# Pacing the row gathers, inverting the routing permutation in bf16, and moving an activation table load in a mixture-of-experts layer

## The reference

```
x = layernorm(x + attention(x))                      # called x1 in the kernel
probs = softmax(x @ gate_w)                          # 1024 x 8
gate_score, gate_idx = top_k(probs, 2), scores divided by their sum
combine[t, e] = gate_score of expert e for token t, times alpha[e]
h = gelu(x @ fc1_w[e] + fc1_b[e])                    # 256 -> 256, per expert
y = h @ fc2_w[e] + fc2_b[e]
x = layernorm(x + sum over e of combine[t, e] * y)
```

## Time and profile before

| | us |
|---|---|
| runs, median of 3 (lowest to highest) | 154.54 (153.67 to 154.86) |
| the profiled execution, in all | 154.99 |
| its span, first to last instruction | 153.2 |
| busy in the span: TensorE products | 119.4 (78%) |
| busy: DVE | 69.8 (46%) |
| busy: ACT | 63.4 (41%) |
| busy: POOL | 50.9 (33%) |
| mean granted TensorE clock | 0.871 of full |

### The profile page before, as it was taken

The page is one execution under the profiler, slowest core; times in us unless marked ns, Lnnn a source line. Parts: engine busy times, 40 slices in busy tenths (PEclk is TensorE's granted clock), DMA queues, the critical chain, the costliest instruction groups (busy, mean ns, idle before and its releaser), DMA issues.

```text
span 153.2 us, 2179 instructions
## 1 busy us (share of the span) xinstructions
PE 119.4 (78%) x682; PEld 102.2 (67%) x682; DVE 69.8 (46%) x202; ACT 63.4 (41%) x156; POOL 50.9 (33%) x75
## 2 busy tenths in 40 slices
PE   7699997989789979993921999999999999910000
PEld 7488896868689979972720878888888888700000
DVE  0559785986817797182011333433322212210981
ACT  4346983454710000354003456656575453500271
POOL 2009993670000001787772000025254354340000
PEclk9999999999955696899598579999999999995555
DMA  4899999902320000233332000000211112117724
GB/s 124 194 369 409 381 348 348 295 15 81 121 76 0 0 0 0 75 103 103 103 103 68 0 0 4 0 34 34 73 36 68 68 39 71 68 68 258 290 101 173
DMA packets 10633, 18.00 MB, mean 118 GB/s; under 512 B 1205, under 2 KB 7550, under 8 KB 10366
## 3 DMA queue, kind: packets, MB, share of 16 engines
q1 hardware_dynamic: 9086, 13.67, 26.2%
q0 software_dynamic: 1536, 4.20, 8.5%
HBM read 13.67 MB, written 4.19 MB: 117 GB/s over the span
## 4 chain that ended last, share of the span: by engine, by line
PE 52%; DVE 11%; issue 10%; DMA 9%; POOL 8%; ACT 5%; SPq 3%; ACTq 0%; POOLq 0%; DVEq 0%
PE ps L1089 16%; PE ps L1077 15%; PE ps L1087 5%; DMA wq<-in_w_q_t 5%; PE ps L913 3%; PE ps L1041 3%; DMA gT_hi<-pair_rows 2%; PE ps L1060 2%; PE ps L981 2%; POOL x L358 2%; DVE acc L876 2%; DVE stats L881 2%; POOL x L357 2%; DMA pair_rows<-kv,scatter_i 2%; SPq L292 2%
## 5 line engine op out<-in xcount | busy, mean ns | idle before, releaser
L530 ACT ACTIVATE g<-ps,b_step 128x128 f32<-128x128 f32 x46 | 14.4, 364 | 36.2 <-PE ps L1077 23.5
L397 POOL DMA_INDIRECT pair_rows<-kv,scatter_i x16 | 15.6, 972 | 39.4 <-DVE kv L862 39.4
L1077 PEld LDWEIGHTS ps<-early,w_now 128*128 128x128 f32 x184 | 25.3, 201 | 4.3 <-issue 2.8
L1077 PE MATMUL ps<-early,w_now 128*128 (+1 forms) x184 | 25.9, 287 | 2.5 <-issue 2.4
L1089 PE MATMUL ps<-wres,g 128*128 x92 | 27.8, 428 | 0.0
L862 DVE SCALAR_TENSOR_TENSOR kv<-ps,w_step,kv 128x256 f32 x23 | 11.1, 483 | 34.0 <-PE ps L1089 33.2
L1089 PEld LDWEIGHTS ps<-wres,g 128*128 128x128 f32 x92 | 16.8, 203 | 4.7 <-issue 0.7
L913 PE MATMUL ps<-ones 128*128 128x128 f32 x102 | 18.2, 355 | 1.0 <-POOL ones L337 1.0
L546 ACT COPY w_now<-wres 128x512 f32 x23 | 14.0, 617 | 11.1 <-issue 11.1
L913 PEld LDWEIGHTS ps<-ones 128*128 128x128 f32 x102 | 17.3, 265 | 1.3 <-POOL ones L337 1.0
L390 POOL DMA_INDIRECT gT_hi<-x_rows,gather_i x8 | 8.5, 1063 | 28.2 <-DVE gather_i L816 26.1
(11 more groups left out here) (157 smaller groups left out, 194.7 us busy)
## 6 DMA issues: line engine op xcount, KB each, us to landing
wres<-in_expert_w SPq DMA_DIRECT2D x8, 512.0 KB, 9.6
early<-in_x_t SPq DMA_DIRECT2D x4, 256.0 KB, 6.0
acc<-in_x_tok SPq DMA_DIRECT2D x1, 1024.0 KB, 9.0
rT<-in_rope_t SPq DMA_DIRECT2D x1, 1024.0 KB, 10.3
x_rows<-x SPq DMA_DIRECT2D x4, 256.0 KB, 2.8
gT_hi<-pair_rows SPq DMA_DIRECT2D x2, 512.0 KB, 4.2
gT_lo<-pair_rows SPq DMA_DIRECT2D x2, 512.0 KB, 6.0
out<-z SPq DMA_DIRECT2D x4, 256.0 KB, 2.2
```

Source lines behind the costliest of these rows:

```text
L397: g_.indirect_dma_start(out=pair_rows[:, :], out_offset=bass.IndirectOffsetOnAxis(ap=scatter_i[:, i:i + 1], axis=0), in_=y_acc[:, i * D:(i ...
L530: a.activation(g[:, s % 2, m, :], two(H_BANK, s)[:, tile(m)], ACT.Gelu, bias=b1_step[:, s, m:m + 1]).then_inc(g_ok, 1)
L1077: last = nc.tensor.matmul(two(H_BANK, s)[:, tile(m)], w1_now[:, s % W1_SLOTS, k, tile(m)], x[:, tile(k)], start=k == 0, stop=k == KD - 1)
```

## The change

1. ACT: the dummy activation that loads the GELU table moves behind the copies of tiles 4 and 6.
2. `WARM_ROUTE` from (10, 12, 4, 14) to (7, 8, 8, 4).
3. The inversion goes in two parts, in bf16. `lane_hot` is bf16 now. First only numbers: lane, token tile and choice of each pair (`ids`, small integers that bf16 holds exactly), by one `tile_id` operation ahead of each `lane_hot`. `gather_i` = lane x 8 + tile, made right behind the product, ahead of the plan; `scatter_i` = 2 x gather_i + choice, later. The weights follow in a second set of 16 products, each float32 weight as a sum of three bf16 parts; these products stand on TensorE between x_across(1) and fc1(0), and DVE adds the three results.
4. The weights' operations (`wt`, `w_of`) move out of the chain ahead of the positions, behind the plan.
5. On DVE x_evict(0) comes ahead of the bias operations, x_evict(1) behind them, and x_evict(2) ahead of DVE's register loads. ACT loads 3 registers, copies three weights, then loads the other 20.
6. POOL: gather i from 4 on waits for xs_ok i - 2, the eviction of tile i - 3. The scatters wait for `scatter_ok`.

```diff
-WARM_ROUTE = (10, 12, 4, 14)
+GATHERED_FIRST = 4
+WARM_ROUTE = (7, 8, 8, 4)
...
-            g_.tensor_copy(values[:, :, 0], pair_id).then_inc(ids_ok, 1)
+            g_.tensor_copy(ids[:, :, 0], own_lane.to_broadcast([P, 2 * T])).then_inc(ids_ok, 1)
+            g_.tensor_copy(ids[:, :, 1], tile_no).then_inc(ids_ok, 1)
+            g_.tensor_copy(ids[:, :, 2], choice_no).then_inc(ids_ok, 1)
...
             for i in range(TS):
+                if i >= GATHERED_FIRST:
+                    pool.wait_ge(xs_ok, i - GATHERED_FIRST + 2)
                 gather(i)
+            pool.wait_ge(scatter_ok, 1)
             for i in range(TS):
                 scatter(i)
...
-            a.activation(table_unused[:, 0:1], eps[:], ACT.Gelu)
             x1_across(4)
             x1_across(6)
+            a.activation(table_unused[:, 0:1], eps[:], ACT.Gelu)
...
-            e_off = loaded(ACT_ENGINE, w_off, (E - 1) * D, "counts of E - 1 comparisons")
+            e_off = loaded(ACT_ENGINE, w_off, (E - 1) * D, "counts of E - 1 comparisons", 0, W1_SLOTS)
...
             for s in range(W1_SLOTS):
                 w1_copy(s)
+            e_off += loaded(ACT_ENGINE, w_off, (E - 1) * D, "counts of E - 1 comparisons", W1_SLOTS, STEPS)
...
-            dve.wait_ge(th_ok, 1)
-            v.tensor_scalar(wt[:, 0, :], th[:], 0.5, 0.5, ALU.mult, ALU.add)
-            step(v.tensor_scalar(wt[:, 1, :], th[:], -0.5, 0.5, ALU.mult, ALU.add))
-            dve.wait_ge(ids_ok, 1)
-            step(v.tensor_tensor(values[:, :, 1], wt[:].rearrange("p k t -> p (k t)"), alp_of[:], ALU.mult))
...
-            v.tensor_tensor(tile_val[:], tile_hot[:].unsqueeze(2).to_broadcast([P, 2 * T, 2, TS]),
-                            values[:].unsqueeze(3).to_broadcast([P, 2 * T, 2, TS]), ALU.mult).then_inc(tile_val_ok, 1)
+            dve.wait_ge(ids_ok, 3)
             for i in range(0, 2 * T, 4):
+                v.tensor_tensor(tile_id[:, i:i + 4, :, :], tile_hot[:, i:i + 4, :].unsqueeze(2).to_broadcast([P, 4, 3, TS]),
+                                ids[:, i:i + 4, :].unsqueeze(3).to_broadcast([P, 4, 3, TS]), ALU.mult).then_inc(tile_id_ok, 1)
                 v.tensor_tensor(lane_hot[:, i:i + 4, :], lane.unsqueeze(1).to_broadcast([P, 4, P]),
...
+            dve.wait_ge(th_ok, 1)
+            v.tensor_scalar(wt[:, 0, :], th[:], 0.5, 0.5, ALU.mult, ALU.add)
+            v.tensor_scalar(wt[:, 1, :], th[:], -0.5, 0.5, ALU.mult, ALU.add).then_inc(w_side, 1)
+
+            dve.wait_ge(inv_mm, 1)
+            lane_ps, tile_ps, choice_ps = (ps[:, INV_BANK, c * TS:(c + 1) * TS] for c in range(3))
+            v.tensor_scalar(slot_lane[:], lane_ps, float(T), None, ALU.mult).then_inc(route, 1)
+            steps[0] += 1
+            dve.wait_ge(route, steps[0])
+            v.tensor_tensor(gather_i[:], slot_lane[:], tile_ps, ALU.add).then_inc(idx_ok, 1)
...
-            dve.wait_ge(inv_mm, 1)
-            step(v.tensor_copy(scatter_i[:], ps[:, INV_BANK, 0:TS]))
-            v.tensor_scalar(gather_i[:], scatter_i[:], 1, None, ALU.logical_shift_right).then_inc(idx_ok, 1)
             v.tensor_scalar(y_off[:], tau_s[:], float(D), None, ALU.mult).then_inc(y_off_ok, 1)
-            step(v.tensor_scalar(odd_i[:], scatter_i[:], 1, None, ALU.bitwise_and))
-            v.tensor_scalar(first[:], odd_i[:], -1.0, 1.0, ALU.mult, ALU.add).then_inc(first_ok, 1)
+            v.tensor_scalar(first[:], choice_ps, -1.0, 1.0, ALU.mult, ALU.add).then_inc(first_ok, 1)
+            dve.wait_ge(idx_ok, 1)
+            v.scalar_tensor_tensor(out=scatter_i[:], in0=gather_i[:], scalar=2.0, in1=choice_ps,
+                                   op0=ALU.mult, op1=ALU.add).then_inc(scatter_ok, 1)
...
+            dve.wait_ge(w_side, 1)
+            w_step_of(v.tensor_tensor(w_of[:], wt[:].rearrange("p k t -> p (k t)"), alp_of[:], ALU.mult))
+            w_step_of(v.tensor_copy(w_parts[:, :, 0], w_of[:]))
+            w_step_of(v.tensor_tensor(w_rest[:, 0, :], w_of[:], w_parts[:, :, 0], ALU.subtract))
+            w_step_of(v.tensor_copy(w_parts[:, :, 1], w_rest[:, 0, :]))
+            w_step_of(v.tensor_tensor(w_rest[:, 1, :], w_rest[:, 0, :], w_parts[:, :, 1], ALU.subtract))
+            w_step_of(v.tensor_copy(w_parts[:, :, 2], w_rest[:, 1, :]))
+            v.tensor_tensor(tile_w[:], tile_hot[:].unsqueeze(2).to_broadcast([P, 2 * T, 3, TS]),
+                            w_parts[:].unsqueeze(3).to_broadcast([P, 2 * T, 3, TS]), ALU.mult).then_inc(tile_w_ok, 1)
+
             v.tensor_scalar(pick_b2[:], eps_s[0:BIAS_ROWS, :], row_e[0:BIAS_ROWS, :], None,
                             ALU.is_equal).then_inc(pick_ok, 1)
...
+            x_evict(0)
             plan_step(v.tensor_tensor(eps_hot[:], eps_s[:].unsqueeze(2).to_broadcast([P, STEPS, E]),
...
             v.reduce_sum(b1_step[:], b1_part[:], axis=AX_X).then_inc(b1_ok, 1)
-            v.tensor_copy(w_slot[:], ps[:, INV_BANK, TS:2 * TS])
...
-            x_evict(0)
             x_evict(1)
+            dve.wait_ge(w_mm, 1)
+            w_high, w_mid, w_low = (ps[:, W_BANK, c * TS:(c + 1) * TS] for c in range(3))
+            plan_step(v.tensor_copy(w_slot[:, 0, :], w_high))
+            plan_step(v.tensor_tensor(w_slot[:, 1, :], w_slot[:, 0, :], w_mid, ALU.add))
+            plan_step(v.tensor_tensor(w_slot[:, 0, :], w_slot[:, 1, :], w_low, ALU.add))
...
+            x_evict(2)
             dve.wait_ge(y_off_ok, 1)
             offs = loaded(DVE, y_off, (TS - 1) * D, "step less counts of experts begun, capped at the last tile")
...
             for s in range(STEPS + 1):
-                if 2 <= s + 2 < TS:
+                if 3 <= s + 2 < TS:
                     x_evict(s + 2)
...
-            pe.wait_ge(tile_val_ok, 1)
             for i in range(2 * T):
+                pe.wait_ge(tile_id_ok, i // 4 + 1)
                 pe.wait_ge(hot_ok, i // 4 + 1)
...
             x_across(0)
             x_across(1)
+            pe.wait_ge(tile_w_ok, 1)
+            for i in range(2 * T):
+                last = nc.tensor.matmul(ps[:, W_BANK, 0:3 * TS], lane_hot[:, i, :],
+                                        tile_w[:, i, :, :].rearrange("p a j -> p (a j)"),
+                                        start=i == 0, stop=i == 2 * T - 1)
+            last.then_inc(w_mm, 1)
```

More of the change, by code:

```diff
@@ L87, in table @@
             return tab[:, at[0] - n:at[0]]
-        before_me, lane, tile_start, pair_id = table(P), table(P), table(TS), table(2 * T)
+        before_me, lane, tile_start, tile_no, choice_no = table(P), table(P), table(TS), table(2 * T), table(2 * T)
         base_mask = table(E * E).rearrange("p (e f) -> p e f", e=E)
@@ L158, in layer_kernel @@
         tile_hot = sb("tile_hot", [P, 2 * T, TS])
-        values = sb("values", [P, 2 * T, 2])
-        tile_val = sb("tile_val", [P, 2 * T, 2, TS])
+        lane_hot = sb("lane_hot", [P, 2 * T, P], BF16)
+        ids = sb("ids", [P, 2 * T, 3], BF16)
+        w_of = sb("w_of", [P, 2 * T])
+        w_rest = sb("w_rest", [P, 2, 2 * T])
+        w_parts = sb("w_parts", [P, 2 * T, 3], BF16)
+        tile_id = sb("tile_id", [P, 2 * T, 3, TS], BF16)
+        tile_w = sb("tile_w", [P, 2 * T, 3, TS], BF16)
         scatter_i = sb("scatter_i", [P, TS], I32)
+        slot_lane = sb("slot_lane", [P, TS])
         gather_i = sb("gather_i", [P, TS], I32)
-        odd_i = sb("odd_i", [P, TS], I32)
         first = sb("first", [P, TS])
-        w_slot = sb("w_slot", [P, TS])
+        w_slot = sb("w_slot", [P, 2, TS])
         start_i = sb("start_i", [P, E], I32)
@@ L189, in layer_kernel @@
         xs = early
-        lane_hot = rT[:].rearrange("p a s -> p (a s)").rearrange("p (i c) -> p i c", i=2 * T)
         y_acc = kv[:].rearrange("p t d -> p (t d)")
@@ L225, in layer_kernel @@
             sem(n) for n in "ident0 ident_ok const_ok all_ones_ok earlier_ok ids_ok b2_hi_ok b2_ok".split())
-        lg_mm, route, gap_ok, th_ok, chosen_ok, pos_mm, tile_val_ok, hot_ok, inv_mm, idx_ok, first_ok, plan, w_off_ok, y_off_ok, pick_ok, b1_ok, w_step_ok = (
-            sem(n) for n in "lg_mm route gap_ok th_ok chosen_ok pos_mm tile_val_ok hot_ok inv_mm idx_ok first_ok plan w_off_ok y_off_ok pick_ok b1_ok w_step_ok".split())
+        lg_mm, route, gap_ok, th_ok, chosen_ok, pos_mm, tile_id_ok, hot_ok, inv_mm, idx_ok, scatter_ok, tile_w_ok, w_mm, first_ok, plan, w_off_ok, y_off_ok, w_side, pick_ok, b1_ok, w_step_ok = (
+            sem(n) for n in "lg_mm route gap_ok th_ok chosen_ok pos_mm tile_id_ok hot_ok inv_mm idx_ok scatter_ok tile_w_ok w_mm first_ok plan w_off_ok y_off_ok w_side pick_ok b1_ok w_step_ok".split())
         w1_now_ok, xs_mm, xs_ok, fc1_mm, g_ok, fc2_mm, acc0_ok, y_ok = (
@@ L267, in layer_kernel, with loaded @@
         X1T_BANK = (2, 3, 0, 2, 3, 0, 2, 3)
-        LG_BANK, POS_BANK, INV_BANK, WARM_BANK = 1, 4, 5, 6
+        LG_BANK, POS_BANK, INV_BANK, WARM_BANK, W_BANK = 1, 4, 5, 6, 4
         def x1T_before(t):
             return (t + 1) // 2, t // 2
-        def loaded(engine, row, most, reason):
```

(17 more changed lines are left out.)

13 lines of the change are left out of this document (9 added, 4 removed).

## The result

| | before | after |
|---|---|---|
| median of 4 runs each on one chip, us | 154.7 (153.67 to 155.13) | 140.67 (138.57 to 140.81) |
| ratio | | 0.9033, 95% interval 0.8896 to 0.9171 |
| profiled execution, us (span) | 154.99 (153.2) | 140.7 (138.8) |

The change is 9.7% faster, 14 us where 11 were forecast. Applied to the 154.54 of the prediction the ratio gives 139.6, just under its low end of 140. The ratio takes only the runs of each kernel that fell in its faster state (138.57 and 140.64 us of the four after); the medians alone would give 0.909 and 140.5.

What follows compares the result with a forecast made beforehand. TensorE work was 52% of the chain, with 10.7 us lost to apparently late semaphore increments. 2.3 us ahead of fc1(2) plus 9.0 behind it made 11.3 less than 154.99: 143.7, given as 143.5 (139.5 to 146; scored range 140 to 148.5).

Steps and rivals of the forecast that it cites:

- the half clock at the loop's start: TensorE, thin stretch from 56 on: slow end 62.6 taken for x_across(0), plus 1.2 us for one half-clock stretch before fc1(5).
- the weight products: Sixteen bf16 products between x_across(1) and fc1(0) on TensorE: cost 0.5 to 0.9 us; fc1(0) at 64.3, 1.7 earlier.
- fc1(2)'s distance: DVE around the first steps: fc1(2) keeps 6.3 us from the eviction of tile 0, so 70.0, 2.3 earlier.
- The stall: fc1(2) to fc1(5): back-to-back gathers make TensorE's semaphore increments late; pacing them saves 9.0 us behind fc1(2).
- Ahead of fc1(2): Routing, planning and first steps up to fc1(2): 2.3 us earlier in all.
- Table load: ACT's GELU table load moved behind the copy of tile 4: gates and logits 0.7 us earlier.
- Inversion: Routing inversion in bf16 on DVE and TensorE: net gain 1.5 us, so inv_mm 3.2 earlier, at 56.1.
- pick_ok and four warm rounds: TensorE ahead of x_across(0): pick_b2 ends 4.8 us from inv_mm, four rounds take 1.1 to 1.8; x_across(0) at 62.0 to 62.8.
- B: Rival, 7%: stall isn't the gathers' spacing, 152.5 us; elsewhere the machine condition with before at 145 to 147 us.
- A: Rival, 12%: pacing relieves only half the stall, 148.2 us; elsewhere the machine condition with before at 154 to 155 us.
- C: Rival, 4%, slower: late increments come with any gather in flight, and pacing stretches the flights; 160 us at 1.5 per gather.
- The rule on the SBUF port: DVE operations lock GpSimd out, so DMA descriptors come late: first gather could lose 2 to 3 us more, some 146 total.

Runs made afterwards that it cites:

- r_before: The kernel before, no edit, for its own trace in the condition where it takes 145 to 147 us: 146.11 us, ratio 1.0049.
- r_after2: The changed kernel, no edit, with more rounds, where the kernel before takes 145 to 147 us: 140.11 us, ratio to before 0.9614.
- r_after: The changed kernel, no edit, where the kernel before takes 145 to 147 us: 141.93 us, ratio to before 0.9828.
- e_table_back: The changed kernel with the dummy GELU activation ahead of ACT's copies of tiles 4 and 6 again: 141.81 us, ratio to before 0.9808.
- e_old_warm: The changed kernel with WARM_ROUTE back at (10, 12, 4, 14), where the kernel before takes 154 to 155 us: 145.09 us, ratio to before 0.9373.

## Why the prediction was right or wrong, point by point

**What put the number outside the range: the half clock at the loop's start.** fc1(5) was forecast at 79.1 and came at 75.75. Of these 3.35 us 1.6 lie behind fc1(2): I added 1.2 for a stretch at half clock and 0.5 for late gathers and evictions, and neither came. The other 1.8 are the balance of what lies ahead of fc1(2): 0.6 because pick_b2 ended earlier, 0.6 because the four warm-up rounds took 1.13 us where I took the slow end of 1.1 to 1.8, and 0.8 because the weight products ran under the eviction of tile 0, an overlap that I had put at nothing; less 0.2 in fc1(2)'s distance from fc1(0). "I take the slow end, 62.6, as TensorE has little to do from 56 on and its granted clock fell to half after other thin stretches" is the step that failed. The clock did stand at half, but from 55.5 to 59.0 us, ahead of the four rounds, and it was full from 59.0 through the whole start of the loop.

**The stall (the main term, 9.0 us).** For the two profiled executions the size holds: fc1(2) to fc1(5) shrank from 17.96 to 7.54 us, the remote waits beside the gathers are gone, and the gathers are released one by one. But I took a stall that needs the machine's condition for one of the kernel alone. The second step that failed is "My reading: back-to-back gathers cause the late increments", as a full cause. Back-to-back gathers aren't sufficient: r_before and three unpaced runs have them in B, and no stall. That in A they are what the increments are late for fits every trace taken there, down to the small delays beside the changed kernel's own short series; whether the pacing is the cure in A was never tested by itself. I call it argued, not shown. That the forecast came within 3 us of the result owes something to luck: the changed kernel was measured against runs in A, and in B the same change gains 2 to 4%. I saw nothing in the trace of one execution that told me; three runs within 1% of each other did not either, since they shared the condition.

I also read two standstills of TensorE as one stall. The first (69.84 to 72.26) is in r_before too, 2.29 us of waiting for the eviction of tile 2 behind DVE's register loads. Only the second, 6.1 us, and the 2.8 us of half clock behind it need A. The other 1.6 us of half clock, between the two, come in B as well.

**Ahead of fc1(2): 2.3 forecast, 4.05 measured.** The chain was right; sizes and one overlap were off.
- *Table load*, 0.7. The copy of tile 4 came 1.8 us earlier, and gate(4) ran at 41.52 still at full clock, 0.51 us instead of 1.02 at half. base_part came 2.9 earlier instead of 1.8. That this is the move's doing isn't shown: in B the gates end at different times from trace to trace (the first DVE operation on the logits at 42.93 in r_after2, 44.76 in r_before, 45.41 in r_after), with the clock, and e_table_back shows no difference.
- *Inversion*, 1.5. From base_part to gather_i before 8.17 us, after 7.11, so 1.1. The tile_id operations cost what I had (0.27 from start to start, forecast 0.25), and lane_hot in bf16 is not faster, as assumed (0.60 from start to start). The missing 0.4 lie behind them: the last four products ended 0.7 us behind the last lane_hot, where I had 0.3.
- *pick_ok and four warm rounds*, then the weight products. The chain was right: pick_b2 ended 4.9 us behind the inversion's product (4.8 forecast), and the rounds ran behind it. The sixteen products took 0.56 us, under the eviction of tile 0 (61.84 to 62.26). fc1(0) started 0.06 us behind that eviction, where I had added 0.5 to 0.9 for them. So fc1(0) came 3.7 us earlier and not 1.7.
- *fc1(2)'s distance* from the eviction of tile 0: 5.95 us instead of 6.33 (forecast 6.3). It waited 1.16 us for the eviction of tile 2, as described.

**The rivals.** B said that then only the gain ahead of fc1(2) remains. In condition B that is nearly what happens: 5.9 us, 4.2 ahead of fc1(2). Its cause as I gave it, that each gather costs as before, isn't it. The Trainium skill, "Runtime: NRT & Kernel Launch", section "Instruction fetch mechanics", was the rule behind it: r_before executes the same instructions without the stall, so fetching alone doesn't make it. A fetch even falls in that stretch in r_before (queue, packets, MB and share, from 66 to 84 us), where the trace before has none:

```profile
q8 instruction: 1, 0.02, 0.4%
```

A foresaw late increments where gathers and scatters are mixed. They are there in A, by 1.5 us beside the first scatters, but only around step 13 and at no cost; the 4.5 us of A are refuted. C, that any gather in flight makes increments late, is refuted: paced ones don't in A, and pacing costs nothing in B.

**The rule on the SBUF port** (the Trainium skill, "SBUF — State Buffer", section "SBUF: two separate sides"). The first four gathers, amid DVE's planning, took 1.19, 0.96, 1.51 and 0.95 us, 0.8 more in sum than four of 0.95. That agrees in kind with the lock it describes; the 2 to 3 us that I priced did not come, and gather 0 wasn't what x_across(0) waited for.

**The half clock.** I expected the thin stretch from 56 to 60 to lower the clock for the start of the loop. The granted clock was 0.66 of 2.4 GHz on average from 55.4 to 60.4, part of the time at the lower level, and 1.00 from 60.4 on, earlier than I assumed. In r_before it fell in the loop once, at fc2(1) and fc1(3), behind TensorE's wait for the eviction of tile 2. These products took 1.7 us longer, as much as the 1.6 us that the change gains behind fc1(2) in B. In e_old_warm ahead of the loop it stood at half again.

## What to carry to other kernels

Before a stall that no line of the profile explains is made the main term of a forecast, run the same kernel in another session: here the same code had it in two sessions and not in five. Cheap insurance against it can be worth having: pacing prefetches a few steps ahead cost nothing where it wasn't needed, here with a slack of 7.4 us against 2.7 to 3.5 from issue to landing. And work put in front of a waiting instruction costs only what sticks out from under the other wait of the next one: sixteen small products beside an eviction were free, while the old warm-up counts, with fourteen rounds in place of four behind a late semaphore, cost 4 us.

## What the runs showed of the hardware that I had not expected

- One kernel, one core, two levels: 152.4 to 155.7 us in two sessions, 143.6 to 148.7 in the others, with nearly all of the difference in one place: fc1(2) to fc1(5) takes 17.96 us in the one and 9.16 in the other. In the slower one the landing records of GpSimd's DMAs are partly missing from the trace.
- In the slower one TensorE's semaphore increments reached ACT late beside GpSimd's back-to-back DMAs: by 9.0 us with sixteen in a row, by 0.7 to 0.8 with five, by 0.4 to 0.5 with three, and by at most 0.3 elsewhere in the changed kernel.
- A second stream of DMA (16 x 256 KB) beside indirect gathers changed the time of the kernel before by 0.4% (interval -0.2 to 1.1%). With the same stream the changed kernel took 141.04 us, against 140.67 without it in the session of the result.
- In condition B single runs of one kernel still differ by 2 to 3% (r_before 144.88 to 148.66), together with a granted clock of 0.866 to 0.893. A move worth 1 us needs more rounds than were run here.
